# Landing-paced GpSimd transfers, a second set of open pages and one TensorE signal a pass in a routed expert kernel

## The reference, cut to what matters

```python
scores = jax.nn.sigmoid(xt @ gate_w.T)
_, idx = lax.top_k(scores + gate_b, TOPK)          # TOPK = 4 of 16 experts
w = take_along_axis(scores, idx, -1); w = w / sum(w) * 2.5
for e in experts:                                  # inner width 128
    y += comb[:, e] * (silu_and_mul(xt @ w13[e].T) @ w2[e].T)
y += silu_and_mul(xt @ w13_s.T) @ w2_s.T
out = xn_source + s * silu(y)                      # s: the recurrent branch
```

## Time and profile before

| | |
|---|---|
| median of three timed runs | 443.7 us (442.36 to 444.87) |
| span of the profiled execution, first to last instruction | 513.9 us |
| TensorE (PE) busy | 339.1 us, 66% |
| VectorE (DVE) busy | 311.1 us, 61% |
| GpSimd (POOL) busy | 265.4 us, 52% |
| ScalarE (ACT) busy | 251.0 us, 49% |
| mean granted clock of TensorE | 0.837 of full speed |

### The profile page before, as it was taken

The page is one execution under the profiler, slowest core; times in us unless marked ns, Lnnn a source line. Parts: engine busy times, 40 slices in busy tenths (PEclk is TensorE's granted clock), DMA queues, the critical chain, the costliest instruction groups (busy, mean ns, idle before and its releaser), DMA issues.

```text
span 513.9 us, 10001 instructions
## 1 busy us (share of the span) xinstructions
PE 339.1 (66%) x3107; PEld 261.7 (51%) x3107; DVE 311.1 (61%) x977; ACT 251.0 (49%) x462; POOL 265.4 (52%) x278
## 2 busy tenths in 40 slices
PE   0365566849467786976799968797876968645210
PEld 0352443626355665755698846575654756433100
DVE  4899776676703545545643626786776555346745
ACT  1851666536434455443787746565664644422000
POOL 2005377766646566655600165766555554436773
PEclk9976698797876889888999989999997898676555
DMA  7998499425443566654779768899977777436653
GB/s 247 305 328 281 129 343 331 161 86 201 143 165 127 175 186 201 196 172 156 216 220 269 227 192 268 281 282 285 285 243 211 249 217 225 128 119 194 174 160 126
DMA packets 88675, 109.27 MB, mean 213 GB/s; under 512 B 9649, under 2 KB 78002, under 8 KB 88626
## 3 DMA queue, kind: packets, MB, share of 16 engines
q1 hardware_dynamic: 74656, 74.47, 45.7%
q0 software_dynamic: 12288, 33.57, 20.7%
q10 hardware_dynamic: 1682, 0.59, 0.4%
HBM read 55.91 MB, written 52.69 MB: 211 GB/s over the span
## 4 chain that ended last, share of the span: by engine, by line
PE 35%; another core or an unknown queue 12%; issue 10%; ACT 8%; DVE 6%; POOL 5%; DMA 1%; ACTq 1%; POOLq 0%; DVEq 0%
PE bank L850 13%; PE bank L872 8%; PE bank L656 6%; POOL xn_parts L638 5%; PE bank L863 3%; ACT xn_f L1851 3%; PE bank L898 2%; ACT sh_h L1868 1%; ACT y_ring L1875 1%; ACT xn_f L1859 1%; ACT x_ring L1881 1%; PE bank L948 1%; DVE mix_sb L1371 1%; PE bank L774 1%
## 5 line engine op out<-in xcount | busy, mean ns | idle before, releaser
L638 POOL DMA_INDIRECT xn_parts<-y_slots,slot_u x128 | 127.2, 994 | 126.2 <-PE bank L656 39.6
L619 POOL DMA_INDIRECT x_slots<-xn_parts,slot_u x128 | 131.7, 1029 | 115.1 <-DVE slot_u L1253 36.0
L850 PE MATMUL bank<-w_all,xn_f 128*128 (+1 forms) x864 | 122.2, 295 | 22.2 <-issue 11.5
L850 PEld LDWEIGHTS bank<-w_all,xn_f 128*128 128x128 f16 x864 | 87.3, 106 | 44.8 <-issue 30.6
L1524 DVE SCALAR_TENSOR_TENSOR xn_f<-bank,xn_f 128x256 f32<-128x256 f32 x72 | 30.5, 424 | 111.9 <-ACT xn_f L1859 69.3
L1851 ACT ACTIVATE xn_f<-bank 128x1024 f16<-128x1024 f16 x72 | 73.5, 1022 | 36.7 <-remote 22.3
L872 PE MATMUL bank<-w_all,sh_silu 128*128 (+1 forms) x432 | 68.2, 299 | 5.5 <-ACT y_ring L1875 4.2
L1875 ACT ACTIVATE y_ring<-bank 128x512 f32<-128x512 f32 x72 | 42.9, 596 | 54.4 <-PE bank L872 33.7
L1859 ACT ACTIVATE xn_f<-bank 128x256 f32<-128x256 f32 x72 | 27.5, 382 | 55.0 <-remote 32.4
L656 PE MATMUL bank<-ident_h,w_stage 128*128 128x128 f16 x576 | 48.6, 231 | 1.5 <-issue 1.4
L872 PEld LDWEIGHTS bank<-w_all,sh_silu 128*128 128x128 f16 x432 | 41.8, 106 | 14.5 <-issue 7.5
(11 more groups left out here) (215 smaller groups left out, 456.9 us busy)
## 6 DMA issues: line engine op xcount, KB each, us to landing
w_stage<-x_slots SPq DMA_DIRECT2D x72, 256.0 KB
y_slots<-y_ring SPq DMA_DIRECT2D x72, 256.0 KB
x_slots<-zero_h SPq DMA_DIRECT2D x10, 1024.0 KB
x_ring<-in_x SPq DMA_DIRECT2D x32, 256.0 KB
w_stage<-in_w13t SPq DMA_DIRECT2D x17, 256.0 KB
x_ring<-in_x SPq DMA_DIRECT2D x8, 512.0 KB, 7.7
out<-mix_sb SPq DMA_DIRECT2D x15, 256.0 KB
w_stage<-in_w2t SPq DMA_DIRECT2D x17, 128.0 KB
```

Of the source, the lines that this page charges most:

```text
L619: eng.indirect_dma_start(out=x_slots, out_offset=bass.IndirectOffsetOnAxis(ap=slot_u[:, n * TOPK + k:n * TOPK + k + 1], axis=0), in_=xn_pa ...
L638: eng.indirect_dma_start(out=fin_y[:, r, j, k, :], out_offset=None, in_=y_slots[0:2 * READY_PAIR[c] * P, :], in_offset=bass.IndirectOffset ...
L850: mm = eng.matmul(gu[:, j * 2 * F:(j + 1) * 2 * F], xg_T[:, n % 2, ((j * 2 + px) * KD + k) * P:((j * 2 + px) * KD + k + 1) * P], weights_o ...
```

## The change

Pages: each of the first two phases gets open pages of its own, so there are 160 pages and 80 pairs. The first phase's 16 full pairs and its 8 open pairs come first; the second phase's certain full pages follow from pair 24, its open pages, which the third phase goes on to fill, from pair 32. The page arithmetic of the second phase becomes that of the first.

Signals: TensorE increments one semaphore, `pair_pass`, at the end of each pass, and all others of the pair loop wait for the pass in which their product was made. The loop has one stage more (down matmuls of pair n - 3, transposes of pair n + 3, 83 passes), the scan takes one step a pass (passes 1 to 28), mix steps begin at pass 40, units come every four passes.

GpSimd: from scatter 63 on, each scatter waits until the last but one has landed. Before each two gathers, the two before the last two must have landed (not for the last four units). The waits on the pair loop go.

```diff
-PAGES = MAIN_PAGES + EXPERTS
+PAGES = MAIN_PAGES + 2 * EXPERTS
...
-    OPEN_AT = KNOWN[1]
-    PAIRS = [*range(E, E + OPEN_AT, 2), *range(0, E, 2), *range(E + OPEN_AT, PAGES, 2)]
+    OPEN = [0, E + KNOWN[1]]
+    PAIRS = [*range(E, E + KNOWN[0], 2), *range(0, E, 2), *range(E + KNOWN[0], PAGES, 2)]
     NPAIR = len(PAIRS)
-    PHASE_PAIR = [0, KNOWN[0] // 2, KNOWN[1] // 2]
-    FILL_PIECES = [(first, first + 8) for first in range(E + KNOWN[1], PAGES, 8)]
-    FILLED_AHEAD = (0, 4, len(FILL_PIECES))
+    PHASE_PAIR = [0, (E + KNOWN[0]) // 2, (E + KNOWN[1]) // 2]
+    FILL_PIECES = [(first, first + 8) for first in range(OPEN[1], PAGES, 8)]
+    FILLED_AHEAD = (0, 6, len(FILL_PIECES))
...
-    XB_RING, YS_RING, AHEAD = 6, 5, 5
+    XB_RING, YS_RING, AHEAD = 6, 5, 6
+    X_AHEAD, H_BEHIND, DOWN_BEHIND = 3, 1, 3
+    PASSES_OF_PAIRS = NPAIR + DOWN_BEHIND
...
-    PER_HEAD_STEP, PER_HALF_SCATTER, PER_HALF_GATHER = 1.4, 1.65, 1.3
+    PER_HEAD_STEP, OUT = 1.4, 2
...
-        SCAN0 = [6, 24]
-        SHIFT = {21: 0, 48: 1}
+        SCAN_PASS = (1, 2 + WARM)
+        SHIFT_PASS = tuple(first + steps for first, steps in zip(SCAN_PASS, STEPS))
...
-        CHECK, FALLBACK, PARTS = 50, 54, 55
-        UNIT_PAIR = tuple(40 + 10 * c // 3 for c in range(10))
-        STATES_SLOT = 86
+        CHECK, FLAG, FALLBACK, PARTS = 85, 87, 90, 91
+        UNIT_PAIR = tuple(40 + 4 * c for c in range(10))
+        STATES_SLOT = 110
...
-        MIX_SLOT = {93 + 6 * c: c for c in range(NU)}
+        MIX_SLOT = {120 + 6 * c: c for c in range(NU)}
...
+        def passed_after(n):
+
+            return n + 3
+
+        def paced_count(i):
+
+            return 16 * ((i - HEAD_SCATTERS) // OUT + 1)
...
-            def half_pair(h):
-
-                if h % 2:
-                    eng.wait_ge(pair_gu, h // 2 - 1)
-                else:
-                    eng.wait_ge(pair_t, h // 2)
+            def slotted(i):
+
+                return x_slotted[i // (BT * TOPK)] if i < HEAD_SCATTERS else x_paced[(i - HEAD_SCATTERS) % OUT]
+
+            def gathered_before(q):
+
+                c, k = q // TOPK, q % TOPK
+                eng.wait_ge(y_in[c % FIN_RING][k], 16 * FT * (c // FIN_RING + 1))
...
-                elif i >= HEAD_SCATTERS:
-                    half_pair(SCATTER_HALF + int((i - HEAD_SCATTERS) / PER_HALF_SCATTER))
...
+                elif i >= HEAD_SCATTERS + OUT:
+                    eng.wait_ge(x_paced[(i - HEAD_SCATTERS) % OUT], paced_count(i - OUT))
...
-                    beside_gather(c * FT * TOPK + i)
+                    if i % FT == 0 and c * TOPK + k >= 2 and c < NU - ROW_UNITS:
+                        gathered_before(c * TOPK + k - 2)
...
-            for n in range(NPAIR + 2):
-                if n + 2 < NPAIR:
-                    pair_x(n + 2)
+            pair_x(2).then_inc(pair_pass, 1)
+            for n in range(PASSES_OF_PAIRS):
                 beside(SLOTS * n)
                 if n + 1 < NPAIR:
-                    pair_up(n + 1)
+                    last = pair_up(n + 1)
                 beside(SLOTS * n + 1)
-                if 1 <= n <= NPAIR:
-                    pair_h(n - 1)
+                if n + X_AHEAD < NPAIR:
+                    last = pair_x(n + X_AHEAD)
+                if 0 <= n - H_BEHIND < NPAIR:
+                    last = pair_h(n - H_BEHIND)
                 beside(SLOTS * n + 2)
-                if n >= 2:
-                    pair_y_down(n - 2)
+                if (step := scan_place(n)) is not None and n > 1:
+                    last = scan_step(*step)
+                if n in SHIFT_PASS:
+                    scan_shift(SHIFT_PASS.index(n))
+                if n >= DOWN_BEHIND:
+                    last = pair_y_down(n - DOWN_BEHIND)
+                last.then_inc(pair_pass, 1)
...
-                eng.wait_ge(pair_t, n + 1)
-                if n >= 2:
-                    eng.wait_ge(pair_gu, n - 1)
-                else:
+                eng.wait_ge(pair_pass, passed_after(max(n - X_AHEAD, -2)))
+                if n < 2:
                     eng.wait_ge(x_lo, NB)
...
-                eng.wait_ge(pair_gu, n + 1)
+                eng.wait_ge(pair_pass, passed_after(n - 1))
...
-                eng.wait_ge(pair_down, n + 1)
+                eng.wait_ge(pair_pass, passed_after(n + DOWN_BEHIND))
```

More of the change, by code:

```diff
@@ L305, in recurrent_gated_moe @@
         x_slotted = [sem(f"x_slotted{b}") for b in range(NB)]
+        x_paced = [sem(f"x_paced{i}") for i in range(OUT)]
         xb_in = [sem(f"x_block_in{i}") for i in range(XB_RING)]
@@ L412, in under, with batch_slotted @@
             return [max(w for w in range(E + 1) if w % STAGES == i) for i in stages]
+        def passed_after(n):
+            return n + 3
+        def paced_count(i):
+            return 16 * ((i - HEAD_SCATTERS) // OUT + 1)
+        def batch_slotted(eng, b):
+            first, end = b * BT * TOPK, (b + 1) * BT * TOPK
+            if first < HEAD_SCATTERS:
+                eng.wait_ge(x_slotted[b], 16 * (min(end, HEAD_SCATTERS) - first))
+            for i in range(max(first, HEAD_SCATTERS, end - OUT), end):
+                eng.wait_ge(x_paced[(i - HEAD_SCATTERS) % OUT], paced_count(i))
         def y_landed(n):
@@ L821, in weights_of @@
             def weights_of(b, first, end):
-                if b < E:
-                    return w_all[:, b, first:end]
+                for opened in OPEN:
+                    if opened <= b < opened + E:
+                        return w_all[:, b - opened, first:end]
                 return w_all[:, bass.ds(expert_value[b], 1), first:end]
@@ L834, in pair_x @@
                     eng.wait_ge(xT_lo, NB)
-                transposed(n % 2, lambda j: x_blk[:, xb_at(n), j // 4, (j % 4) * P:(j % 4 + 1) * P], 8, pair_t)
+                tb = TP[n % 2][:, :].bitcast(f16)
+                for j in range(8):
+                    t = eng.transpose(tb[:, j * P:(j + 1) * P], x_blk[:, xb_at(n), j // 4, (j % 4) * P:(j % 4 + 1) * P],
+                                      ident_h[:, :])
+                return t
             def pair_up(n):
@@ L845, in pair_up @@
                     b = PAIRS[n] + j
-                    if b >= E and b % VL == 0:
+                    if b % VL == 0 and not any(opened <= b < opened + E for opened in OPEN):
                         load_experts(b)
@@ L1415, in _ @@
                 route_rows(g)
-            room_first()
             pages_passed(0)
@@ L1675, in _ @@
             pair_up(0)
-            for n in range(NPAIR + 2):
-                if (step := scan_place(SLOTS * n)) is not None:
+            pair_split(0)
+            for n in range(PASSES_OF_PAIRS):
+                beside(SLOTS * n)
+                if (step := scan_place(n)) is not None:
                     scan_sum(*step)
-                beside(SLOTS * n)
-                if (step := scan_place(SLOTS * n + 1)) is not None:
-                    scan_sum(*step)
+                if n in SHIFT_PASS:
+                    scan_shift(SHIFT_PASS.index(n))
+                if 0 <= n - H_BEHIND < NPAIR:
+                    pair_h(n - H_BEHIND)
                 if n + 1 < NPAIR:
                     pair_up(n + 1)
-                if n < NPAIR:
-                    pair_split(n)
+                    pair_split(n + 1)
                 beside(SLOTS * n + 1)
-                if 1 <= n <= NPAIR:
-                    pair_h(n - 1)
                 beside(SLOTS * n + 2)
@@ L1912, in _ @@
             pair_up(0)
-            for n in range(NPAIR + 2):
-                if n + 2 < NPAIR:
-                    pair_x(n + 2)
+            pair_x(2)
+            pair_split(0)
+            for n in range(PASSES_OF_PAIRS):
                 beside(SLOTS * n)
+                if n >= DOWN_BEHIND:
+                    pair_y_out(n - DOWN_BEHIND)
                 if n + 1 < NPAIR:
                     pair_up(n + 1)
-                if n < NPAIR:
-                    pair_split(n)
-                beside(SLOTS * n + 1)
+                if (step := scan_place(n)) is not None:
+                    beside(SLOTS * n + 1)
+                    scan_step(*step)
+                if n + X_AHEAD < NPAIR:
+                    pair_x(n + X_AHEAD)
+                if n + 1 < NPAIR:
+                    pair_split(n + 1)
+                if scan_place(n) is None:
+                    beside(SLOTS * n + 1)
                 beside(SLOTS * n + 2)
-                if n >= 2:
-                    pair_y_out(n - 2)
             for c in range(len(UNIT_PAIR) - 1, NU - 1):
```

270 lines of the change are left out of this document (111 added, 159 removed).

## The result

The changed kernel takes 499.2 us (495.4 to 503.5, four runs), the kernel before 443.7 us beside it: ratio 1.124, 95% interval 1.118 to 1.129. It is 55.5 us slower, where the text on record expected 440 us and faster. Its profiled execution has a span of 497.5 us, 1.7 under its time. Where the runs of a version fall into two groups, the time and ratio given are those of the faster group: for d3 the runs of 448.4 and 450.1 us beside 457.6 and 457.9, while the texts on record count from the median of all four, 453.9.

The account below looks back on a forecast made before the run. Runs of GpSimd's transfers, not DMA load, were taken to hold up the loop, at least under the profiler. 147.6 + 120.8 + 139.4 + 42.9 = 450.7, less 13, plus 2 of stalls: 439.7, so 440 us; range 427 to 458.

Parts of the forecast that it names:

- The stalls: Pair loop: about 12 us of stalls in the timed runs that the change can remove, 2 of them left.
- h: Head: how much of its 22.5 us of unexplained waits the timed runs lack; 0 to 22.5, taken as 13.
- rival B: Loop: the stalls are the profiler's, h is near 0 and the pairs are paid in full: 449 us; chance 0.14.
- The floor: Whole kernel before, without stalls: head 149, first part 110.3, second part 139.4, tail 46.4, in all 445.1 us.
- Second part, by VectorE: Loop passes 31 to 73 before: VectorE's pass, mix and unit work, 3.61 us where all meet, over TensorE's 2.64.
- Eight pairs: Loop's first part, up to the mix steps: nine more passes, 23.8 us of TensorE's time, but only 10.5 us longer.
- Scatters, 1.45 us each: First part, GpSimd: two under way cost 2.9 us, so the last starts at 235.6 and pair 32 is loaded at 240.8.
- Rival A: First part: scatters become the bound at 1.8 us each, 23 us more, about 460 us; chance 0.22.
- One signal a pass: Pair loop: TensorE's matmuls stay, its 88 us under the scatters' 91.8; ScalarE and VectorE get a pass of slack.
- Second part unchanged: Passes 40 to 82: VectorE at 3.36 us a pass in 40 to 71, then 11 of 2.9: 139.4 us as before.
- Gathers, four under way: GpSimd's gathers: at 1.27 us each and about 4 us to land they rarely meet the limit; cost nothing.
- Page arithmetic: Head: 15 small operations before group 3's slots become 7, 1.4 us less on VectorE; head 147.6.

Follow-up runs that it names:

- d3: Changed kernel with another VectorE order, places moved a pass, eight scatters under way, no gather limit, units every 3.33 passes: 449.2 us.
- d4: d3 with the changed kernel's limit of four gathers under way put back: 476.0 us.
- b1: Kernel before with eight more pairs, of pages that no row is sent to, after pair 24: 454.2 us, ratio 1.027.
- b3: Kernel before with two scatters under way from the sixty-third on, in place of the half-pair waits: 464.7 us, ratio 1.050.
- d5: d3 with two scatters under way in place of eight: 467.8 us.
- a1: Changed kernel with eight scatters under way in place of two: 495.7 us, ratio 1.120.
- a2: Changed kernel with own signals for the end of pair_up, pair_x and the scan step from pass 3 on: 500.1 us, ratio 1.130.
- c3: Changed kernel with all six kinds of TensorE signal as before from pass 3 on, and a third buffer for transposed hidden rows: 500.1 us.
- d9: d3 with the six signals of c3, its third buffer, and four scatters under way in place of eight: 450.2 us, ratio 1.016.
- d7: d3 with the old places of VectorE's choosing, the passed pages and the scan's flag: 466.1 us.
- d6: d3 with the changed kernel's order on VectorE put back for the second part: 475.4 us.
- c1: Changed kernel with mix and unit operations placed between VectorE's three pair operations from pass 40 on: 485.8 us, ratio 1.092.
- c4: Changed kernel with no limit on how many gathers are under way: 499.7 us.

## Why the prediction was wrong

**The stalls (its last term, 12 us to gain).** This step failed. Its h of 13 us, what the timed runs lack of the head's waits, was right: the same matmuls beside which it cut the head at 149 start 12.7 us sooner in the second profile (timeline, TensorE, first profile and second):

```profile
149.07 0.60 PE L883 MATMUL bank<-ident_f,x_ring 128*128 128x128 f32 x4
```

```profile
136.33 0.60 PE L883 MATMUL bank<-ident_f,x_ring 128*128 128x128 f32 x4
```

But the 12 us of stalls that it then had to have in the loop are not there. From 136.3 to the last y_out at 388.9 are 252.6 us, 2.9 over the floor's 249.7; what is left of the difference is in the tail, 52.3 for 46.4. So next to nothing was there for the change to remove, and the 10 us that the sum lets the change gain are wrong. The rival B, stalls of that profile alone, was right on this, though not on an h near 0; at 449 us it was far off too.

**The floor, 445.1 us.** Right as a number (441.2), with 12.7 us too much in the head, 2.9 too little in the loop and 5.9 in the tail. The last scatter, 218.7 for 230.3, is 11.6 us sooner, which the head accounts for: the 1.27 us a scatter were about right (1.29). What it lacked is what sets the end: GpSimd issues 128 gathers at 1.33 us each behind pair 31's rows, and 33 of them are left at the last y_out. d4 changes their pace alone. "Second part, by VectorE" is a second bound of nearly the same length by its sum; no run sets it apart in the kernel before.

**Eight pairs, 10.5 us in the first part.** Borne out where it was tested, in the kernel before: b1 gives 11.2. Not seen: in the changed kernel the same eight pairs stand ahead of unit 6's gathers, a wait of 12.4 us in d3, which takes back the 4.3 us by which its first gather is earlier, and more.

**Scatters, 1.45 us each.** Mis-sized: 1.77 in the changed kernel, 1.63 in b3, a price of 18.5 (d5) and 21.8 us (b3) where nothing else holds the first part. The one scatter of 2.6 us from start to landing, of the earlier trace rows, was the last, with no other behind it; the median from issue to landing is 3.1 in a1 and 3.5 in b3. Rival A's mechanism and its 1.8 us were right. By the Trainium skill (DMA: Bandwidth & Descriptors, Anatomy of one DMA) a transfer of 131 KB takes an estimated 2.3 us, too low for these medians. That most of the fixed 2.0 us in it is the receipt of the last write, as the Trainium skill says there, no run here shows; that a wait for landing puts the latency into the rate, as the prediction drew from it, b3 and d5 show.

**One signal a pass, "a whole pass of slack for each product".** This step failed. The signal itself costs nothing that these runs tell (a2, c3, d9). What it moves costs 16.9 us (d7): it sets VectorE's side work back by most of a pass, and no slot was moved for it. The forecast looked at what ScalarE and VectorE take from TensorE, and not at what TensorE takes from VectorE.

**Second part unchanged, 3.36 us a pass.** This step failed, and is one of the two dearest: 4.01 us a pass, 26.2 us (d6). 3.36 is a sum of busy times (the trace has 12.06 / 4 = 3.02), and the diff's new order of the three pair operations on VectorE was not costed at all; with the other order c1 takes 13.55 / 4 = 3.39. An engine that waits 1 us a pass with its own work queued behind is at its bound with a quarter of its time idle.

**Gathers, four under way, "cost nothing".** This step failed: 26.8 us (d4), the other of the two dearest, unseen in c4 since pair 55 was late anyway. The forecast held two averages, 1.27 us to issue and 4 to land, against each other. But the limit works by twos: before each two gathers both of the two before the last two must have landed, so one slow gather holds up all behind it. A gather takes 3.9 us in the median in the changed kernel and up to 6.5, and four are issued in 5.1.

**Page arithmetic.** Pair 0's y_out is as before, at 142.9 and 143.0. The loop's first up matmuls start 2.5 us sooner (128.4 for 130.9), and pair 0's result comes a pass later; whether the page arithmetic gave the 2.5 us no run tells.

None of the versions beats the kernel before: d3 and d9, the best with two sets of open pages, are some 1.2% and 1.6% behind it. What the pass of depth and the units every four passes cost by themselves is open.

## What to carry to other kernels

When several queues run in step, find the last engine in the chain (here GpSimd's gathers) and write every edit's cost as what it does to that engine's start, pace and gates. Test repairs together and then take one back at a time: here three repairs out of four gave 0 to 3.5 us alone, and each is worth 17 to 27 us. Before a sum is made from a profile, hold its span against the timed runs, and when they part by far more than the 1.7 us seen here, take another profile.

## What the runs showed of the hardware

Waiting for a transfer's landing before the next is started turned the 1.27 us that a scatter takes GpSimd into 1.63 to 1.77 us with two under way, and the 10.5 us for eight gathers into 13 to 14 with four under way, though the gathers had room by their median, 3.9 us to land for four in 5.1 us of issue.

After a stop of TensorE of 3.0, 4.2 and 8.4 us the next twelve matmuls took 2.65, 2.74 and 2.77 us in place of 1.47, at a granted clock of 0.50 to 0.54 (1.2 for 2.4 GHz is 0.50), so each of these stops cost 1.2 to 1.3 us more than its length in these twelve matmuls alone.

Two profiles of one unchanged kernel spanned 513.9 and 441.2 us, with the same operations equally long on VectorE (424 and 423 ns for L1524). 12.7 of the 72.7 us lie ahead of L883, in the head. No run here explains the longer one.
